# Where the zeros of the last layer's expert regions are written: third attention or wide attention

## The reference, cut to what matters

```
x = x + tanh(g_xattn[0]) * L0_xattn(layernorm(x), ctx)            # 16 heads
x = x + tanh(g_ffn[0])   * L0_ffn(layernorm(x))                   # 4-bit quantised linear
x = x + tanh(g_xattn[1]) * L1_xattn(layernorm(x), ctx, ctx, mask) # 16 heads, rotary
x = x + tanh(g_ffn[1])   * L1_ffn(layernorm(x))                   # top-1 of 8 experts
x = x + tanh(g_xattn[2]) * L2_xattn(layernorm(x), ctx, ctx, mask) # 16 heads
x = x + tanh(g_ffn[2])   * L2_ffn(layernorm(x))                   # top-1 of 8, capacity
x = x + tanh(g_xattn[3]) * L3_xattn(layernorm(x), ctx, ctx)       # ONE head of width 256
x = x + tanh(g_ffn[3])   * L3_ffn(layernorm(x))                   # top-2 of 8 experts

def L3_ffn(x, ...):
    topv, topi = top_k(ffn(x, gate), 2)
    topv = topv / sum(topv)
    return sum over the two chosen experts e of topv[e] * (selu(x @ wi[e] + bi[e]) @ wo[e] + bo[e])
```

## Time and profile before

| | us |
|---|---|
| median of 3 runs (3755.05 to 3758.78) | 3756.08 |
| the profiled execution, its own time | 3761.58 |
| its span, first to last instruction | 3760.4 |
| TensorE busy | 3360.2 (89%) |
| VectorE / ScalarE / GpSimd busy | 2184.2 / 2015.7 / 938.2 |
| mean granted clock of TensorE | 0.944 of full |
| moved by DMA | 456.02 MB, mean 121 GB/s |

### The profile page before, as it was taken

One profiled execution on the slowest core, in us unless ns is written; L12 is line 12 of the kernel. 1 busy time (PEld: TensorE's weight loads), 2 busy tenths in 40 slices (PEclk: granted clock), 3 DMA queues, 4 the chain that ended last, 5 costly groups with the idle time before them and its releaser, 6 DMA issues.

```text
span 3760.4 us, 52430 instructions
## 1 busy us (share of the span) xinstructions
PE 3360.2 (89%) x18396; PEld 1787.4 (48%) x18396; DVE 2184.2 (58%) x3497; ACT 2015.7 (54%) x4454; POOL 938.2 (25%) x1057
## 2 busy tenths in 40 slices
PE   5999999978699999997897989999978979897997
PEld 2333333325333333334695323223327956687996
DVE  5767676847778787883203867767841033364333
ACT  2677766753247677774332466666752322254664
POOL 2232222004456642001202534220002010022332
PEclk8999999989899999998898999999998989998998
DMA  8132323115664433205764665562118421032555
GB/s 197 45 104 69 101 75 95 25 57 179 179 184 117 116 91 88 49 9 169 231 221 145 195 150 140 137 169 61 26 35 302 155 94 53 26 123 103 183 183 170
DMA packets 248063, 456.02 MB, mean 121 GB/s; under 512 B 54059, under 2 KB 151636, under 8 KB 245628
## 3 DMA queue, kind: packets, MB, share of 16 engines
q1 hardware_dynamic: 165542, 225.63, 22.5%
q0 software_dynamic: 55376, 189.97, 16.1%
q10 hardware_dynamic: 26885, 37.07, 3.0%
HBM read 292.46 MB, written 153.91 MB: 119 GB/s over the span
## 4 chain that ended last, share of the span: by engine, by line
PE 75%; DVE 9%; DMA 8%; ACT 2%; POOL 2%; issue 2%; SPq 1%; ACTq 0%; POOLq 0%; DVEq 0%
PE pv L1445 15%; PE s L1431 14%; PE m L1409 13%; PE h L2937 5%; PE y L2945 5%; DVE mxp L1272 4%; PE h L2511 4%; PE y L2520 4%; PE y L1917 3%; PE s L1897 2%; PE s L1373 2%; DMA rc<-z 2%; PE m L1461 1%; DMA qaug<-tm 1%; PE s L1391 1%
## 5 line engine op out<-in xcount | busy, mean ns | idle before, releaser
L1272 DVE TENSOR_REDUCE mxp<-m 128x1 f32<-128x802 f32 x1536 | 1444.9, 987 | 476.4 <-PE m L1409 474.9
L1529 ACT ACTIVATE e_t<-s 128x512 f32<-128x512 f32 (+1 forms) x2496 | 1331.3, 600 | 553.9 <-PE s L1431 549.3
L1431 PE MATMUL s<-qaug,kaug 100*128 100x512 bf16 (+1 forms) x2496 | 837.8, 388 | 35.8 <-DMA qaug<-tm 20.8
L1409 PE MATMUL m<-kaug,qaug 97*128 97x401 bf16 x3072 | 797.8, 343 | 44.9 <-DVE mxp L1272 27.6
L1445 PE MATMUL pv<-e_t,v 128*32 128x512 f32 (+1 forms) x4992 | 675.3, 613 | 0.2
L1431 PEld LDWEIGHTS s<-qaug,kaug 100*128 100x128 bf16 (+1 forms) x2496 | 245.5, 100 | 578.2 <-ACT e_t L1529 364.3
L1409 PEld LDWEIGHTS m<-kaug,qaug 97*128 97x128 bf16 x3072 | 261.5, 99 | 544.6 <-DVE mxp L1272 279.2
L127 POOL TENSOR_TENSOR rstd<-rstd,mhalf 128x4 f32<-128x4 f32 (+2 forms) x12 | 26.5, 2210 | 1090.6 <-DVE rstd L120 1090.6
L3007 ACT ACTIVATE ez<-h,b 128x128 f32<-128x128 f32 x440 | 119.7, 387 | 160.1 <-PE h L2937 160.0
L1445 PEld LDWEIGHTS pv<-e_t,v 128*32 128x32 f32 (+1 forms) x4992 | 99.2, 109 | 216.1 <-ACT e_t L1529 156.7
L2398 DVE SCALAR_TENSOR_TENSOR y<-y,b 128x256 f32<-128x256 f32 x39 | 16.6, 425 | 303.6 <-PE y L2520 303.6
(11 more groups left out here) (392 smaller groups left out, 3831.2 us busy)
## 6 DMA issues: line engine op xcount, KB each, us to landing
w<-in_L_w POOLq DMA_DIRECT2D x78, 1024.0 KB, 5.4
w<-in_L_w SPq DMA_DIRECT2D x24, 1024.0 KB, 13.0
xregion<-zero POOLq DMA_DIRECT2D x10, 2056.0 KB, 16.4
kaug<-kparts SPq DMA_DIRECT2D x16, 1200.8 KB
kaug<-kready SPq DMA_DIRECT2D x32, 600.4 KB
kaug<-kready SPq DMA_DIRECT2D x16, 1200.8 KB
vn<-values SPq DMA_DIRECT2D x8, 1536.0 KB
values<-p_vb ACTq DMA_DIRECT2D x21, 512.0 KB, 5.3
```

The lines of the kernel that those rows point to most:

```text
L1272: dve.tensor_reduce(a.mxp[:, u.g % 2, half, n:n + 1], a.m_slot[u.m % 2][:].rearrange("p (a n) -> p a n", a=2)[:, :, 0:PIECE + 1], AX.XY, A ...
L1409: m = pe.matmul(slot[:, 512 * k:512 * k + PIECE + 1], a.qaug[0:R_MAX, u.g, j, P * qc:P * qc + P], a.kaug[0:R_MAX, u.g, j, k0:k0 + PIECE + ...
L1431: pe.matmul(slot[0:KW[u.k], :], a.kaug[0:R_ALL, u.g, u.j, P * u.k:P * u.k + KW[u.k]], a.qaug[0:R_ALL, u.g, u.j, :], start=True, stop=True) ...
L1529: act.activation(a.e_t[0:KW[u.k], e % 2, u.j, :], a.s_slot[u.s % 3][0:KW[u.k], :], ACT.Exp).then_inc(s_free.sem, 1)
```

## The change

The clears, their tile of zeros and its filling leave the third attention, and with them the wait for their end in that stage's fence. The wide attention gets them: POOL fills the tile, and then issues one transfer each time `y_full` has counted one tile more, for the first 12 of the 16 tiles. The wait for all 12 stands in that stage's fence.

```diff
@@ head_attention
-        a.clears = ready and rope is None
-        if a.clears:
-            a.zero = sb("zero", [P, D + 1])
...
-        cleared = kn.sema("cleared", DMA)
-        kn.fence(*(...), *(((cleared.sem, cleared.at(CLEARED)),) if a.clears else ()),
+        kn.fence(*(...),
@@ head_pool
-    if a.clears:
-        pool.memset(a.zero[:], 0.0)
...
-        elif u.kind == "take" and a.clears and u.b:
-            pool.wait_ge(filled.sem, filled.at(2))
-            clear_pool(kn, a, (u.b - 1) * NG + u.g)
@@ wide_attention
+        a.zero = sb("zero", [P, D + 1])
         wide_sp(kn, a)
+        wide_pool(kn, a)
...
-        kn.fence(*((kn.sema(n).sem, kn.sema(n).base) for n in ("x_done", "t_free")))
+        cleared = kn.sema("cleared", DMA)
+        kn.fence((cleared.sem, cleared.at(CLEARED)), *((kn.sema(n).sem, kn.sema(n).base) for n in ("x_done", "t_free")))
@@ new
+def wide_pool(kn, a):
+    pool, cleared = kn.nc.gpsimd, kn.sema("cleared", DMA)
+    zeros, y_full = kn.sema("zero_made"), kn.sema("y_full")
+    parts = GATED_ROWS // REGION
+    pool.memset(a.zero[:], 0.0).then_inc(zeros.sem, 1)
+    pool.wait_ge(zeros.sem, zeros.at(1))
+    for nth in range(CLEARED):
+        to, lo = (kn.dram["xregion"], REGION * nth) if nth < parts else (kn.dram["yback"], REGION * (nth - parts))
+        width = to.shape[1]
+        pool.wait_ge(y_full.sem, y_full.at(nth + 1))
+        pool.dma_start(to[lo:lo + REGION, :].rearrange("(p r) c -> p r c", p=P),
+                       a.zero[:, 0:width].rearrange("p (a c) -> p a c", a=1).to_broadcast([P, REGION // P, width])).then_inc(cleared.sem, DMA)
```

More of the change, by code:

```diff
@@ L845, in head_attention @@
             ends += ["maskrow", "live_made", "const"]
-        cleared = kn.sema("cleared", DMA)
-        kn.fence(*((kn.sema(n).sem, kn.sema(n).base) for n in ends), *(((cleared.sem, cleared.at(CLEARED)),) if a.clears else ()),
+        kn.fence(*((kn.sema(n).sem, kn.sema(n).base) for n in ends),
                  *(prepare_close(kn, a.p) if a.p else ()))
@@ L1557, in head_spread_act @@
                  kn.dram["sums"].rearrange("j (a n) -> j a n", a=1).to_broadcast([HG, HD, T])).then_inc(summed.sem, DMA)
[L1560 to L1568, removed]
 def s2_step(u):
@@ L1775, in wide_attention @@
         for name, n in (("t_full", a.n_t), ("t_free", a.n_t), ("y_full", QC * B), ("y_free", QC * B),
-                        ("sc_full", QC * B), ("peak", QC * B), ("exped", QC * B), ("x_done", 1)):
+                        ("sc_full", QC * B), ("peak", QC * B), ("exped", QC * B), ("x_done", 1), ("zero_made", 1)):
             kn.sema(name).close(n)
```

## The result

The changed kernel takes **3707.45 us** (median of 4 runs, 3700.09 to 3719.85), the kernel before beside it 3757.43 (4 runs, 3755.05 to 3760.93). The ratio is 0.987, 95% interval 0.984 to 0.9899: 50 us less. The profiled execution of the changed kernel took 3710.9 us, span 3709.7, against a span of 3760.4 before: 50.7 us less.

What follows compares the result with a forecast made beforehand. The kernel was taken as TensorE's work, with time lost where it waits for late small transfers beside clears in the third attention; five terms summed to 54.1 us, 3756.1 - 54.1 = 3702 us, range 3696 to 3721.

Steps and rivals of the forecast that it cites:

- the zero in the wide attention: Wide attention: taking the clears costs 0, since TensorE sets the pace and clears 13 us or more apart don't pile up.
- five terms: Third attention: savings in five stretches disturbed by clears, 1.5, 12.8, 10.1, 13.0 and 16.7 us, 54.1 us in all.
- twin: Stretch with as many matmuls and no clears, taken as the new length of a disturbed third-attention stretch.
- The other stretches keep their time: Third attention: stretches outside the five disturbed ones were to last as long as before, gain 0.
- The cover in the wide attention: Wide attention: clears take 8.9 us at most each, and value loads have 50.4 us of room; cost 0.
- First rival: Third attention turns: not held by clears, so only `rc<-z` waits go; gain 24.4 us, time 3732; chance 0.08.
- Second rival: Third attention: splits' stores and fetches fill the engines themselves, so waits stay, or the edit doesn't relieve them; 3756; chance 0.04.
- the one `rc<-z` of 9.34 us: Ahead of the first clear: a copy of 8.94 us behind the key fetch, beside POOL's stores; its delay was to stay.
- Third rival: Wide attention, L1917: values of batches 2 and 3 come late behind the clears; time about 3764; chance 0.02.

Runs made afterwards that it cites:

- The burst: Changed kernel with all twelve clears issued in a row behind the first tile of the wide attention: 3705.97 us, ratio 0.9865 to the kernel before.
- both sets of clears: Changed kernel with all 12 whole clears done at their old places in the third attention too: 3753.41 us, ratio 0.9999 to the kernel before.
- the clears behind the reciprocal: Kernel before, its clears still in the third attention but each held until VectorE has written `rc` for a given group: 3701.83 us, ratio 0.9855.
- longer pieces at the old places: Kernel before, clears at the same places in pieces of four rows, 4112 bytes instead of 1028: 3732.61 us, ratio 0.9934.
- the clear in four parts: Third-attention clears released by `nm` just ahead of a turn, each cut into four transfers of 512 rows: 3791.19 us, ratio 1.0067 to the kernel before.
- the clears at the turn: Kernel with the reciprocal's wait, its clears released instead by `nm`, just ahead of a turn: 3803.78 us, ratio 1.0121 to the kernel before.

## Why the prediction was right, point by point

**The forecast** was 3702 us, 3696 to 3721; measured were 3707.45. The place (third attention, at the turns), the size (54.1 us forecast from the five stretches, 53.3 from first to last turn) and the zero in the wide attention hold. The median lies 5 us above the forecast; with a first stretch of the second attention that varies by 8 us over traces of the same code, and runs 20 us apart, nothing can be read from that. The 2 to 3 us around the median that I allowed for the spread were too few: one of the four runs, 3719.85, nearly left the range. And that the sum and the turns agree within a microsecond is partly luck: the five terms came to 55.7, and the fifth stretch took 2.4 us back.

**The five terms**, forecast and measured: 1.5 and 2.5; 12.8 and 14.6; 10.1 and 9.0; 13.0 and 13.0; 16.7 and 16.7. The second came out at its upper end. The step behind it was the choice of twin by the count of matmuls: I took the twin with 229 and 39.30 us. In the trace after, the same stretch has 225 and 37.52 us. Over all fifteen stretches both traces have the same 3355 matmuls, so none is missing; a few fall on the other side of a turn. The weight loads, the next column, are 221 before and after, as in the stretches of 37.5 us and in the twin of 39.30, while the stretches of 40.39 us have 229. So they name the kind of stretch better, and of two stretches of one kind the one at clock 1.00 is the clean one; the twin of 39.30 stood at 0.97.

**"The other stretches keep their time"** failed for one: 41.25 us became 43.63, with TensorE waiting for `nm`. It was 42.6 to 43.7 in every trace in which the third stretch lasts 37.5 us and no clear stands at the turns of the fourth and fifth, with clears in the stage or without, and 41.1 to 41.9 where the third lasts 45 to 52. So it goes with the stretches ahead being short, not with the clears being gone. Through which instruction was not found, and stays open.

**The cover in the wide attention** held, and so did its size. I took 8.9 us of the engines' time per clear from five done in 44.4 us. GpSimd's queue (packets, MB, share) in the 195 us from 3020 to 3215, and the stretch from the first clear's issue to the last one's landing:

```profile
q0 software_dynamic: 6336, 25.25, 53.4%
```
```profile
3025.93:3191.50 165.57, 160.38 (x663) 107.99 (x662) 50.61 (x92) 44.56 (x75) 13.48 (x12) 1.00 0.76 193
```

That is 104 us for twelve, 8.7 us each, and a mean DMA share of 0.76, inside the 0.6 to 0.8 forecast; the 0.91 above is a stretch with a load of values beside two clears. Landing takes longer than that, 14.3 us for `xregion` (8.4 for `yback`), and the steps of 13 us and more let each clear land about when the next is issued. The burst shows that the cover would hold even with all twelve at once.

**First rival, the turns are not held by the clears.** It falls with four runs: the loss is back with both sets of clears, it grows by 102 us over the clears behind the reciprocal when they are moved to the turn, and it shrinks with longer pieces at the old places and at the turn. The row was 13.06 us for 4 KB; the rule behind the rival was the turn-taking of the Trainium skill, "DMA: Bandwidth & Descriptors", section "Queues, rings and completion order". By that alone a small transfer would pass. The measurement decides: the first transfer of a turn does get through ahead of the clear's end, but after 5.8 us in place of 1.7, and the third, for which TensorE waits, after 12.5. The same section has a second rule, which I didn't weigh: the semaphore increment that ends a transfer lands only after every earlier write of that DMA engine, across its queues. The pairs that end within 1.3 us of each other agree with it, and so does the clear in four parts, of which three are ahead of the turn's last transfer. No run here separates it from other causes, such as a full path for writes to HBM.

**Second rival, the load stays.** It falls with the stretches after and with both sets of clears. The loads that were there all along are the price only of the one `rc<-z` of 9.34 us, as forecast.

**Third rival, slower by late values.** It falls with the wide stage at 230.46 us, spread out and in a burst.

What I had not seen is that the reason is finer than "clears in flight in this stage". The stretches lasted long because a clear was in flight at a turn or at an `rc<-z`; between them it is free, or nearly (2.3 us once, with two). The clears behind the reciprocal win as much as the change without leaving the stage.

## What to carry to other kernels

In this kernel a large write to HBM cost by its moment and by the time it was in flight, not by its share: put it where no engine is about to wait for a small transfer, and tie its issue to the event behind which the longest quiet piece begins. Make its pieces long (4 KB instead of 1 KB) where that moment can't be had. And cut a loop at its own turns and compare stretch by stretch: the sum of five rows gave the gain of the stage within a microsecond or two, while the average DMA share would have pointed to the wrong stretch.

## What the runs showed of the hardware that was not expected

- 2 MB written from one SBUF tile of zeros took 12.6 to 15.7 us where little else was moving when in rows of 1028 bytes, 8.4 to 8.6 us in rows of 1024 (`yback`), and 9.0 us (median of all twelve) when four rows went as one piece. So four bytes more per row go with half as long again and more; the two tensors differ too, and no run changes the row length alone. In the wide attention the first clear moved 273 GB/s in its first microseconds (3027.5 to 3031) and 206 after them (3031 to 3036), with the engines busy throughout (a share of 0.95 and 1.05); one of `yback` moved 337 GB/s (3167.2 to 3173.4). The issue on GpSimd took 1.11 to 1.16 us for 128 x 16 pieces and 0.75 for 128 x 4.
- Of the three transfers of 4 KB of a turn, issued 0.5 to 1.7 us behind such a write, the first took 5.8 us and the last 12.5, ending 1.3 us before the write landed; without one each takes 1.7 to 1.8.
- TensorE's rate didn't move at all between a DMA share of 0.00 and one of 1.02, while before, and with the clears at the turn, the stretches in which it waited 4 to 10 us at once had a granted clock of 0.84 to 0.92, against 0.97 to 1.00 in the five stretches of the changed kernel: some 18 of the 56 us of the five stretches came from that. The first stretch of the stage stood at 0.89 before and after, with no wait above 0.8 us in it, so a wait is not the only thing that goes with a low clock.
